# An attention block with an FP4 feed-forward on one core: the last head pair's row maxima subtracted by VectorE, and the second pair's transposes in front of the values' first half

## What is computed

```
q = (layernorm(x) @ W_tgt.T + b_tgt) * mask
k, v = split((ctx @ W_src.T + b_src) * mask)
scores = q @ k.T / sqrt(16), -inf where the mask is 0
attn = softmax(scores)          # exp(scores - rowmax) / sum
x = x + concat(layernorm(x), attn @ v) @ W_out.T + b_out
x = x + fp4_ffn(layernorm(x))
```

## Time and profile before

| | us |
|---|---|
| three runs | 204.83, 204.89, 205.24 |
| profiled execution | 205.46 |
| its span in the trace | 203.2 |
| TensorE matmul busy | 185.8 |
| VectorE busy | 174.8 |
| GpSimd busy | 141.2 |
| ScalarE busy | 132.1 |

### The profile page before, as it was taken

The page is one execution under the profiler, slowest core; times in us unless marked ns, Lnnn a source line. Parts: engine busy times, 40 slices in busy tenths (PEclk is TensorE's granted clock), DMA queues, the critical chain, the costliest instruction groups (busy, mean ns, idle before and its releaser), DMA issues.

```text
span 203.2 us, 5834 instructions
## 1 busy us (share of the span) xinstructions
PE 185.8 (91%) x2105; PEld 142.6 (70%) x2105; DVE 174.8 (86%) x383; ACT 132.1 (65%) x280; POOL 141.2 (70%) x206
## 2 busy tenths in 40 slices
PE   5889989999889999999998999689999998999881
PEld 5564866859649788596785775467878676877780
DVE  6558989988998988969868888999999999999861
ACT  2066997959778699696868735485566564656740
POOL 6353691678898685954919577797999966868870
PEclk9999999999999999999999999999999999999997
DMA  5799970401200000000000000000101100110013
GB/s 199 236 239 345 353 250 7 155 5 31 75 3 2 3 3 5 0 0 3 5 3 0 3 2 0 0 5 0 53 0 55 43 9 0 55 50 5 0 59 99
DMA packets 13698, 11.99 MB, mean 59 GB/s; under 512 B 790, under 2 KB 10590, under 8 KB 13670
## 3 DMA queue, kind: packets, MB, share of 16 engines
q1 hardware_dynamic: 13086, 11.23, 18.0%
q10 hardware_dynamic: 584, 0.39, 0.6%
HBM read 9.52 MB, written 2.10 MB: 57 GB/s over the span
## 4 chain that ended last, share of the span: by engine, by line
PE 50%; POOL 18%; issue 12%; DVE 8%; DMA 4%; ACT 4%; SPq 1%; POOLq 0%; ACTq 0%; DVEq 0%
PE bank L1034 7%; PE bank L1125 5%; PE bank L1022 5%; POOL wq_y L391 5%; DMA x_all<-in_x 4%; POOL xn L282 3%; POOL hq L406 3%; PE bank L1093 3%; PE bank L1090 3%; PE bank L985 3%; PE bank L1105 3%; PE bank L1028 3%; PE bank L997 3%; PE bank L971 2%; PE bank L1043 2%
## 5 line engine op out<-in xcount | busy, mean ns | idle before, releaser
L1125 PE MATMUL bank<-wdT,hT 128*128 128x128 f32 x186 | 26.4, 278 | 1.8 <-issue 0.8
L1090 PE MATMUL bank<-guT,xqT 128*128 128x352 f32 x64 | 24.6, 465 | 2.2 <-DVE hh L843 2.2
L1125 PEld LDWEIGHTS bank<-wdT,hT 128*128 128x128 f32 x186 | 23.2, 191 | 3.1 <-issue 1.9
L1093 PE MATMUL bank<-guT,xqT 128*128 128x352 f32 x64 | 24.2, 460 | 0.0
L406 POOL TENSOR_TENSOR hq<-wq_u,sch 128x704 f32<-128x704 f32 x15 | 21.2, 1411 | 3.6 <-DVE wq_u L869 3.5
L391 POOL TENSOR_TENSOR wq_y<-hh,ivh 128x704 f32<-128x704 f32 x15 | 21.1, 1407 | 3.4 <-ACT ivh L620 2.8
L715 DVE TENSOR_REDUCE den<-prob 128x8 f32<-128x512 f32 x32 | 19.8, 667 | 0.0
L614 ACT COPY hT<-bank 128x384 f32<-128x384 f32 x32 | 15.2, 474 | 5.1 <-PE bank L1105 5.1
L1034 PE MATMUL bank<-wsT,cT 128*128 128x128 f32 x128 | 17.6, 281 | 0.8 <-DVE q_m L700 0.8
L843 DVE TENSOR_TENSOR hh<-bank,mask_bc 128x352 f32<-128x352 f32 x32 | 15.9, 496 | 1.6 <-PE bank L1093 1.2
L1034 PEld LDWEIGHTS bank<-wsT,cT 128*128 128x128 f32 x128 | 15.4, 191 | 2.5 <-DVE q_m L700 2.3
(11 more groups left out here) (136 smaller groups left out, 503.8 us busy)
## 6 DMA issues: line engine op xcount, KB each, us to landing
cT<-in_ctxT SPq DMA_DIRECT2D x8, 512.0 KB, 5.2
x_all<-in_x SPq DMA_DIRECT2D x8, 256.0 KB, 6.7
mask_bc<-in_mask_rows SPq DMA_DIRECT2D x8, 256.0 KB, 6.7
out_y<-mask_bc SPq DMA_DIRECT2D x7, 256.0 KB, 2.2
wsT<-in_WsT ACTq DMA_DIRECT2D x1, 256.0 KB, 5.0
out_y<-mask_bc SPq DMA_DIRECT2D x1, 192.0 KB, 2.0
w_all<-in_wg SPq DMA_DIRECT2D x1, 176.0 KB
w_all<-in_wu SPq DMA_DIRECT2D x1, 176.0 KB
```

The source lines that it names most:

```text
L1090: nc.tensor.matmul(gu_bank[2 * n % 3][:, 0:I], xqT[g % 2][:, t], guT[:, 0, :], start=True, stop=True).then_inc(pe_g, 1)
L1093: nc.tensor.matmul(gu_bank[(2 * n + 1) % 3][:, 0:I], xqT[g % 2][:, t], guT[:, 1, :], start=True, stop=True).then_inc(pe_u, 1)
L1125: last = nc.tensor.matmul(bank[:, j * P:(j + 1) * P], hT[n % 2][:, c, :], wdT[:, c, :], start=(c == 0), stop=(c == 2))
```

## The change

VectorE gets a new instruction per step, `minus_max(g2)`, behind `update` and ahead of `block_max`: it reads the scores of pair 3 from PSUM and the row maxima of pair 3 from SBUF, subtracts, and writes the result to the buffer `prob` of pair 3 in SBUF. `exp` of pair 3 then reads that buffer and writes it in place, and waits for VectorE (`sub_ok`) where it waited for TensorE. TensorE's fourth `minus_max` is gone. Apart from that, TensorE's transposes of pair 1 now stand ahead of the first half of the values.

```
+SUB = PAIRS - 1
...
             def exp(g, p):
                 n = g * PAIRS + p
-                act.wait_ge(pe_mm, n + 1)
+                pr = prob[g % 2][p][:, :, :].rearrange("p j c -> p (j c)")
+                if p == SUB:
+                    act.wait_ge(sub_ok, g + 1)
+                    nc.scalar.activation(pr, pr, ACT.Exp, scale=float(HD) ** -0.5).then_inc(p_ok, 1)
+                    return
+                act.wait_ge(pe_mm, g * SUB + p + 1)
...
             def row_max(g, p):
                 n = g * PAIRS + p
                 dve.wait_ge(pe_s, g + 1)
-                past(dve, pe_mm, n + 1 - PAIRS)
+                past(dve, *((sub_ok, g) if p == SUB else (pe_mm, (g - 1) * SUB + p + 1)))
...
+            def minus_max(g):
+                n = g * PAIRS + SUB
+                dve.wait_ge(mx_ok, n + 1)
+                past(dve, pe_T, n + 1 - 2 * PAIRS)
+                past(dve, sum_ok, n + 1 - 2 * PAIRS)
+                nc.vector.tensor_tensor(prob[g % 2][SUB][:, :, :].rearrange("r j (e s) -> r (j e) s", s=S),
+                                        s_bank[SUB][:, :].rearrange("r (h s) -> r h s", s=S),
+                                        mx[SUB][:, :, :].rearrange("r j e -> r (j e)").unsqueeze(2).to_broadcast(
+                                            [P, 2 * TILES, S]),
+                                        ALU.subtract).then_inc(sub_ok, 1)
...
                 if on(g3):
                     update(g3)
+                if on(g2):
+                    minus_max(g2)
                 if on(g4):
                     block_max(g4)
...
                 if on(g2):
                     minus_max(g2, 2)
-                    minus_max(g2, 3)
                     prob_transpose(g2, 0)
+                    prob_transpose(g2, 1)
                 if on(g1) and k > 0:
                     v_project(g1, 0)
                 if on(g2):
-                    prob_transpose(g2, 1)
                     prob_transpose(g2, 2)
```

More of the change, by code:

```diff
@@ L178, in xattn_ffn @@
         pad_ok = sem("pad_ok")
+        sub_ok = sem("sub_ok")
         w_halves = (slice(0, WALL // 2), slice(WALL // 2, WALL))
@@ L509, in exp @@
                 n = g * PAIRS + p
-                act.wait_ge(pe_mm, n + 1)
+                pr = prob[g % 2][p][:, :, :].rearrange("p j c -> p (j c)")
[4 more added lines that the diff above has]
+                act.wait_ge(pe_mm, g * SUB + p + 1)
                 past(act, pe_T, n + 1 - 2 * PAIRS)
                 past(act, sum_ok, n + 1 - 2 * PAIRS)
-                nc.scalar.activation(prob[g % 2][p][:, :, :].rearrange("p j c -> p (j c)"), s_bank[p][:, :], ACT.Exp,
-                                     scale=float(HD) ** -0.5).then_inc(p_ok, 1)
+                nc.scalar.activation(pr, s_bank[p][:, :], ACT.Exp, scale=float(HD) ** -0.5).then_inc(p_ok, 1)
             def probT_evac(g, p):
```

## The result

| | median, us | runs | ratio to before, 95% interval |
|---|---|---|---|
| before | 204.87 | 204.71 to 205.24 | |
| after | 202.84 | 201.2 to 203.66 | 0.9888 (0.9857 to 0.9919) |
| after, measured again on another chip | 202.93 | 202.69 to 204.08 | 0.9897 (0.9866 to 0.9929), before 204.89 |

The change makes the kernel faster by 2.0 to 2.3 us (2.03 and 1.96 between the medians, 2.3 and 2.1 by the ratios); the prediction was 203.0 us. The profiled execution of after took 202.57 us with a span of 200.3 us, against 205.46 and 203.2 before.

What follows compares the result with a forecast made beforehand. TensorE was taken to bound steps 5 to 7, a loop through the other engines nearly as long. Steps 1 to 3 -0.35, step 4 -0.355, steps 5 to 7 -1.185: -1.89 us, giving 203.0 us, range 202.2 to 204.4.

Steps and rivals of the forecast that it cites:

- What bounds the kernel: TensorE alone from step 4 to the end of step 7, 39.7 us; a loop through the other engines nearly as long.
- the one loose place in front of the values: TensorE, between pair 0's transposes and the values: could hand over at 73.00, but the values start at 73.14.
- The wait for `q_masked`: Values on TensorE wait for `q_masked`: 0.14 + 0.09 = 0.23 us a step, to be filled by pair 1's transposes.
- The price of the subtraction: VectorE: 0.60 us start to start, upper 0.67; covered in steps 5 to 7, +0.08 in step 4.
- The wait for `exp` 1: TensorE stands 0.06 us before pair 1's transposes for the second `exp`; steps 5 to 7 gain 0.395 each.
- signs of being wrong: Subtraction over 0.8, TensorE standing over 0.1 for `exp` before pair 1, or `s3_round` right behind `stats1` with ScalarE's result ready.
- Steps 1 to 4: Steps 1 to 3 give -0.35 us together, limited by `q_masked` on VectorE; step 4 gives -0.355.
- larger gain: Rival: L772 slips ahead of L297, the loop gives way in steps 2 and 3 too; -3.0, 201.9 us; chance 0.04.
- Step 8: Step 8 and the feed-forward move as a whole with the last groups' statistics, with no further gain; subtraction covered there.
- The absolute time: Whole kernel: 205.46 - 1.89 = 203.57 for the profiled execution, less 0.57 above the median, gives 203.0 us.

Runs made afterwards that it cites:

- e1: Kernel before with only the transposes of pair 1 moved ahead of the values' first half, all four `minus_max` still on TensorE; 202.18 us, ratio 0.991.
- e2: Kernel before with only the fourth `minus_max` moved from TensorE to VectorE, order of transposes unchanged; 204.2 us, ratio 1.001.
- e10: Changed kernel with ScalarE's `exp` of pairs 0 and 1 put in front of its first key evacuation; 201.51 us, ratio 0.9867 to before.
- e3: Changed kernel with a second subtraction of the same operands on VectorE, written to a spare buffer; 204.55 us, ratio 1.0038 to before.
- e8: Kernel before with GpSimd's step 2 bias addition and step 3 weight multiplication moved behind VectorE's roundings; 203.98 us, ratio 0.9985.
- e9: Kernel before with pair 1's transposes moved and GpSimd's bias addition and weight multiplication behind VectorE's roundings, no VectorE subtraction; 202.13 us, ratio 0.9858.
- e6: Changed kernel with GpSimd's step 3 weight multiplication moved behind the next layer norm's statistics and `s3_round`; 201.76 us, ratio 0.9832 to before.
- e11: Changed kernel with GpSimd's bias addition and weight multiplication later and `exp` 0 and 1 ahead of the key evacuation; 201.66 us, ratio 0.9836 to before.
- e7: Changed kernel with both GpSimd's step 2 bias addition and step 3 weight multiplication behind VectorE's roundings; 201.62 us, ratio 0.9835 to before.
- c1: The changed kernel, unaltered, measured again on another chip; 202.93 us, ratio 0.9897 to before.
- e4: Changed kernel with GpSimd's step 2 bias addition made to wait for VectorE's two weight roundings; 201.07 us, ratio 0.9856 to before.

## Why the prediction was right

**What bounds the kernel** was read rightly. TensorE alone sets steps 5 to 7, and the one loose place in front of the values was worth what it looked like: e1, which does nothing but fill it, has nearly the whole gain.

**The wait for `q_masked`**, 0.14 + 0.09 = 0.23 us a step, is confirmed twice: in e1 it is gone and the steps are 12.58 and 12.61 instead of 12.82 and 12.85 (0.24 less), and in e2, where it stays, the removed product brings nothing.

**The price of the subtraction**, 0.60 from start to start and 0.68 printed, is what the rows show, in all eight (681 to 691 ns). It was covered in steps 5 to 7 and not in step 4, as said: in e2 `q_masked` of step 4 comes 0.06 later than before, counted from the first `q_masked`. In the changed kernel neither the subtraction nor the piece of `xn2_of` beside it is stretched (0.68 and 0.45). The Trainium skill (page SBUF — State Buffer, section Who interferes with whom) has the subtraction, with one SBUF input, free of contention, and the trace agrees.

**The wait for `exp` 1** was the term that was mis-sized. The prediction had "TensorE stands 0.06 here" and nothing else; TensorE lost 0.11, and the steps gave 0.34 to 0.35 instead of 0.395. The period was to be about 12.43 and is 12.49 to 12.51. The weight loads (PEld) show what was left out. After:

```profile
71.33 0.91 PEld L1004 LDWEIGHTS bank<-ident,prob 128*128 128x128 f32 x8 [0.56 <-ACT prob L520]
```

And in e1:

```profile
71.40 1.00 PEld L985 LDWEIGHTS bank<-ident,prob 128*128 128x128 f32 x8
```

In e1 the first weights are loaded at 71.40, 0.20 ahead of the first transpose (71.60), while the fourth `minus_max` runs. In the changed kernel that product is gone, and the first load waits for `exp` of pair 0 (its end is 71.28) and starts together with its transpose at 71.33. The transpose behind it then comes after 0.166 instead of 0.109. The same happens at the fifth, the first of pair 1: its load starts at 71.82, 0.05 behind the end of `exp` 1 (71.77), and the next transpose comes after 0.159. So 0.057 is lost behind `exp` 0 and 0.050 behind `exp` 1, and the two make the 0.107 by which these eight take 0.980 where those of e1 and e10 take 0.873. Steps 6 and 7 show the same two places. The fifth transpose starts 0.057 later than four undisturbed ones would let it, which is the predicted 0.06, and `exp` 1 alone would have held it as long. What the prediction missed is `exp` 0, which now stands directly in front of the first load, and the restart at pair 1. It had noted such a restart for the values (0.99 instead of 0.90 behind a wait) and didn't charge it to the transposes. One of its signs of being wrong was a stand for `exp` in front of pair 1 of more than 0.1. Directly there it is 0.05 to 0.06; counted over both restarts, 0.107 is just over that line. e10 took the whole loss away and got back 0.10 a step.

**Steps 1 to 4** gave 0.85 instead of 0.705. The prediction let L772 "start at the same place or just after L297". It started 0.08 ahead of it, and the pair ended 0.26 earlier in the span, 0.1 of that net of the earlier start; this is the condition of the "larger gain" rival, but it brought 0.1 (step 2 in the table) and not the 1.1 between -1.89 and -3.0, because the second piece was then held instead of the first. The prediction also put `q_masked` of step 2 down to VectorE alone; in the kernel before, TensorE came as late there, by a gap of 0.72 that it didn't name (the query projection ends at 32.79 and `q_masked` starts at 32.83).

**Step 8** "moves as a whole" failed, to the good side, by 0.24. ScalarE in step 8 before:

```profile
110.47 0.60 ACT L513 ACTIVATE prob<-a_pair 128x512 f32<-128x512 f32 x1
...
116.33 0.63 ACT L524 ACTIVATE a<-y 128x512 f32<-128x512 f32 x1
```

And after:

```profile
108.26 0.63 ACT L515 ACTIVATE prob<-prob 128x512 f32<-128x512 f32 x1 [0.24 <-DVE prob L723]
...
114.15 0.63 ACT L530 ACTIVATE a<-y 128x512 f32<-128x512 f32 x1
```

There TensorE is not dense: each `minus_max` waits 0.21 for its row maxima, and the transposes stood behind the fourth (109.35); now they stand behind the third (106.72), 2.63 earlier. `exp` 3 comes 2.21 earlier, held by the subtraction, and `a` 2.18, against 2.03 at the first `minus_max` of step 8 (107.33 and 105.30): 0.15 for the removed product, where steps 5 to 7 got 0.10 each. A last 0.10 comes from L754, which took 0.82 before and its counterpart 0.70 after (from `s3_round` of step 8 to the last residual sum it is 81.71 before and 81.61 after). That part is not clearly the change's: it is a meeting with GpSimd's `xn2_of`, and L754 or its counterpart also took 0.82 to 0.84 in e3, e8 and e9 and 0.69 to 0.72 in all the others. e1 and e2 bear the split out: behind step 7 the move alone gains 0.08, all of it with L754, and the subtraction alone 0.23, of which 0.15 comes ahead of it. The same rows show a small miss of the other sign: `exp` 3 does wait for the subtraction there, 0.24, where the prediction had it covered.

**The absolute time** came out right, 202.84 against 203.0, partly by errors that cancel: 0.155 too much for steps 5 to 7 and 0.145 too little for steps 1 to 4. What is left is the 0.24 of step 8. In the spans the change looks like 2.9 us, of which 0.16 at the start and 0.6 at the last transfer are not its doing.

**What stays open.** Why the first `q_masked` starts up to 0.77 us earlier or later, and why the last transfer of 64 KB lands after 1.6 in some executions and 3.8 in others. In the profiled executions the time less the work reaches from 16.44 (e8) to 18.99 (e6), a spread of 2.55 us outside the work. That could make up the up to 2.9 us by which the runs of one kernel differ here, but only one execution per measurement has a trace, so that it does in the others is an inference. Open are also the gaps of TensorE in steps 2 and 4 that nothing releases. In the two profiles of the changed kernel they are 0 and 0.35 in step 2, and 1.02 and 0.59 in step 4, and the work still agrees within 0.08, since VectorE comes last in both places; where TensorE comes last, as in step 2 of e9, they count.

## What to carry to other kernels

Before an instruction is taken off a full engine, look at what stands behind it: in front of a wait it is worth nothing (e2), and the cheaper edit is the one that puts ready work in front of the waiting one (e1). Look also at what it covered: the product that is gone here had hidden the wait for the first `exp`. When a profile is compared with another, find two events between which all the changed work lies, and read the distance; the span had 0.76 us in it that belonged to the start and the last store. And an instruction moved between VectorE and GpSimd can change who starts first at a meeting far behind it, so two edits that each help need not add up (e11).

## What the runs showed of the hardware

- When a VectorE instruction with two SBUF inputs and a GpSimd instruction overlap, in the pairs shown here the one that had started first kept its normal time, and the other was stretched: GpSimd's addition 1.94 instead of 1.28 us, the fourth piece of its normalisation 0.95 instead of 0.45, its 128 x 4 instruction 0.72 instead of 0.20; VectorE's `s3_round` 2.13 to 2.57 instead of 0.69. (In e7 L261 came first and lasted only 0.20, and neither was stretched.) I had expected only VectorE to pay. The Trainium skill (page SBUF — State Buffer, section Who interferes with whom) says that the order of issue decides who blocks, and by that these pairs agree. Where the printed starts lie close, they don't always tell who wins: in step 8 of e1 a piece of `xn2_of` started 0.14 us ahead of L754 and took 0.99 instead of 0.45, while L754 kept 0.69; before, with 0.16 us, it kept 0.45 and L754 took 0.82.
- An f32 tensor in PSUM minus a broadcast bf16 operand in SBUF costs VectorE the same 0.68 us for 128 x 512 as two f32 operands.
- The restart of TensorE behind a wait costs 0.05 to 0.06 us in a list of transposes (0.166 and 0.159 to the next one instead of 0.109) and 0.09 in front of the values, beyond the wait itself. The weight load does not run ahead of the wait: behind a wait it starts with its matmul (71.33 in step 5 after), and in the rows without a wait 0.10 to 0.21 ahead of it.
- In step 4 TensorE stands in the middle of `attend` with nothing that releases it (1.02 after, 0.59 in c1, 0.28 in e1, 1.15 in e4), and in some profiles in the middle of the key projections of step 2. No run here explains it.
